# A transformer block with top-1 experts: token rows stored unsorted in f32 with their gate, and gathered by an inverse permutation made with one-hot matmuls

## What is computed

```python
mod = (_silu(L0_c) @ L0_wmod).reshape(L0_c.shape[0], 6, 1, -1)
sa, ca, ga, sb, cb, gb = (mod[:, 0], ...)          # ga, gb: size at least 0.25
h = _layernorm(x, axis=-1) * (1 + ca) + sa
x = x + ga * attention(h, Wqkv, bqkv, Wout, bout)
h = _layernorm(x, axis=-1) * (1 + cb) + sb
# feed-forward, on the 2048 rows of h:
logits = h @ router_w.T
scores = sigmoid(top-1 logit at its expert, -inf elsewhere)
xr = h[None, :, :] * scores.T[:, :, None]
gate, up = split(einsum('eth,ehf->etf', xr, gate_up_proj))
routed = einsum('etf,efh->eth', up * silu(gate), down_proj)
shared = silu(h @ shared_gate_w) * (h @ shared_up_w) @ shared_down_w
x = x + gb * (shared + routed.sum(axis=0))
```

## Time and profile before

| | us |
|---|---|
| median of 3 runs | 487.85 |
| profiled execution | 487.16 |
| its span, first to last instruction | 485.4 |
| TensorE busy | 401.1 (83%) |
| VectorE busy | 327.2 (67%) |
| GpSimd busy | 235.0 (48%) |
| ScalarE busy | 224.3 (46%) |

### The profile page before, as it was taken

One profiled execution on the slowest core, in us unless ns is written; L12 is line 12 of the kernel. 1 busy time (PEld: TensorE's weight loads), 2 busy tenths in 40 slices (PEclk: granted clock), 3 DMA queues, 4 the chain that ended last, 5 costly groups with the idle time before them and its releaser, 6 DMA issues.

```text
span 485.4 us, 8469 instructions
## 1 busy us (share of the span) xinstructions
PE 401.1 (83%) x2960; PEld 227.5 (47%) x2960; DVE 327.2 (67%) x619; ACT 224.3 (46%) x385; POOL 235.0 (48%) x267
## 2 busy tenths in 40 slices
PE   4738779899988999789986995777568999999991
PEld 4215335444654465444444452444345666666660
DVE  3779899557969879995678459959914444544431
ACT  2512325677566758466865661736601232222320
POOL 1482943653348713672247535428730555565542
PEclk9978999999999999999999999799969999999998
DMA  8563155736600663111222102518674343322320
GB/s 255 173 160 86 48 112 121 245 95 175 157 0 4 144 153 123 43 47 36 88 88 86 46 1 86 165 54 276 235 222 139 64 84 73 66 43 49 48 39 0
DMA packets 41319, 50.12 MB, mean 103 GB/s; under 512 B 5336, under 2 KB 36444, under 8 KB 41280
## 3 DMA queue, kind: packets, MB, share of 16 engines
q1 hardware_dynamic: 36096, 42.34, 30.5%
q0 software_dynamic: 5184, 7.25, 7.4%
HBM read 33.75 MB, written 16.75 MB: 104 GB/s over the span
## 4 chain that ended last, share of the span: by engine, by line
PE 55%; DVE 16%; POOL 8%; ACT 6%; DMA 6%; issue 6%; SPq 1%; DVEq 0%; POOLq 0%; ACTq 0%
PE bank L1341 33%; PE bank L1455 5%; PE bank L1439 5%; PE bank L1411 4%; DVE W L1115 3%; PE bank L1672 2%; DVE x_sb L1070 2%; DVE mx L1026 2%; POOL W L660 2%; ACT W L788 2%; PE bank L1413 2%; DMA boutb<-in_bout 1%; ACT W L813 1%; DMA qk_d<-W 1%; DVE W L1068 1%
## 5 line engine op out<-in xcount | busy, mean ns | idle before, releaser
L813 ACT ACTIVATE W<-bank 128x512 f32<-128x512 f32 (+1 forms) x176 | 95.0, 563 | 63.5 <-PE bank L1439 61.9
L1026 DVE TENSOR_REDUCE mx<-bank 128x1 f32<-128x384 f32 (+3 forms) x176 | 104.8, 631 | 22.8 <-PE bank L1413 22.2
L1341 PE MATMUL bank<-W 128*128 128x256 f16 (+2 forms) x756 | 108.0, 296 | 12.2 <-POOL W L654 3.4
L1341 PEld LDWEIGHTS bank<-W 128*128 128x128 f16 x756 | 74.2, 101 | 46.2 <-issue 12.4
L679 POOL TENSOR_SCALAR_AFFINE_SELECT W<-W 128x512 f32<-128x512 f32 x64 | 43.8, 687 | 83.0 <-ACT W L813 83.0
L1411 PE MATMUL bank<-W 126*128 126x128 f16 (+3 forms) x256 | 65.0, 309 | 14.0 <-DMA W<-qk_d 8.0
L1341 PE MATMUL bank<-W,h2T 128*128 x276 | 68.5, 385 | 1.3 <-issue 0.7
L1439 PE MATMUL bank<-W 128*128 128x512 f16 (+3 forms) x256 | 62.3, 304 | 2.5 <-ACT W L813 2.0
L756 POOL DMA_INDIRECT out<-h2T,row x23 | 36.4, 1582 | 56.8 <-DVE h2T L1310 56.5
L1455 PE MATMUL bank<-W 128*32 128x128 f32 (+3 forms) x512 | 47.5, 444 | 3.1 <-POOL W L679 3.1
L1341 PE MATMUL bank<-h2T,W 128*128 128x512 f16 x192 | 44.5, 384 | 5.2 <-DVE W L1130 5.2
(11 more groups left out here) (154 smaller groups left out, 560.6 us busy)
## 6 DMA issues: line engine op xcount, KB each, us to landing
stage<-in_gup SPq DMA_DIRECT2D x14, 512.0 KB
qk_d<-W SPq DMA_DIRECT2D x48, 128.0 KB
W<-qk_d SPq DMA_DIRECT2D x32, 192.0 KB, 4.2
stage<-in_down SPq DMA_DIRECT2D x7, 512.0 KB
row<-xs_d SPq DMA_DIRECT2D x23, 130.0 KB, 2.6
xs_d<-fillb SPq DMA_DIRECT2D x2, 1040.0 KB, 5.2
x_sb<-in_x SPq DMA_DIRECT2D x4, 512.0 KB, 9.0
out<-x_sb SPq DMA_DIRECT2D x4, 512.0 KB, 3.7
```

The lines of the kernel that those rows point to most:

```text
L813: a.activation(PT[j][:, i:i + m, :], t_bank(N)[:, 0:m * w].rearrange("p (i n) -> p i n", i=m), ACT.Exp).then_inc(s_exp, 1)
L1026: v.tensor_reduce(mx_v[:, b % 2, hp0 // 4, par, i:i + m, t], SB[N % 3][:, 0:m * w].rearrange("p (i n) -> p i n", i=m), AX.X, ALU.max).then ...
L1341: i = t_.matmul(outp, l, r, start=(n == 0), stop=(n == len(prods) - 1), **kw)
```

## The change

- Rows go to memory unsorted. A token's row in `h2_d` is 2 KB: 256 f32 values of h2 already multiplied by the sigmoid weight, and 256 f32 gate values gb. The gate halves of all rows are written once, in batch 0. The h2 halves are made by POOL (`rows`) in the attention loop, two batches behind, and by ACT for batch 3; SP stores them (`rows_out`).
- The weight of batches 0 to 2 is computed as 1 / (1 + exp(-top)) with ACT's exp and DVE (`expo`, `score`), that of batch 3 with the sigmoid as before.
- The high and low f16 parts of the rows, the zero fill, the 16 scatters, the loads of sorted tiles and the gathers of gates are gone. h2 is transposed in f32 (`h2_turn`), and its parts are made out of PSUM (`h2_high`, `h2_low`).
- `slots` makes, for every token, a one-hot of its tile (times its row number plus 1) and a one-hot of its row in the tile (`ohv`, `ohl`); 16 matmuls (`inverse`) turn them into the row number at every sorted place. `places` makes the gather and scatter indices. POOL then gathers the sorted tiles straight from `h2_d`, 8 buffers deep.
- In the routed stage two f32 transposes of a tile take the place of four f16 ones; ACT copies the high part (`rows_in_high`), DVE subtracts for the low one (`rows_in_low`).
- `POOL_UNITS` grows from 4 to 9 units, `ffn_splits` is another row of numbers, `hidden_low(n - 1)` stands right behind `hidden(n)`, and the jobs of batch 3 stand in another order.

```diff
-POOL_UNITS = (9, 11, 13, 15)
+POOL_UNITS = (9, 11, 13, 15, 17, 19, 21, 23, 25)
...
-        (27, "scale2", -1, 1), (28, "parts2", -1, 0), (29, "scale2", -1, 2), (29, "qk", 2, 2),
-        (30, "parts2", -1, 1), (31, "scale2", -1, 3), (31, "qk", 2, 3), (33, "parts2", -1, 2),
-        (35, "parts2", -1, 3), (20, "bias", 0, 0), (38, "h2", -1, 0), (40, "h2", -1, 1),
-        (42, "route", -1, 0)]
+        (27, "scale2", -1, 1), (29, "scale2", -1, 2), (29, "qk", 2, 2),
+        (31, "scale2", -1, 3), (31, "qk", 2, 3),
+        (20, "bias", 0, 0), (37, "h2", -1, 0), (39, "h2", -1, 1),
+        (42, "route", -1, 0), (2, "expo", -2, 0), (4, "score", -2, 0), (6, "rows", -2, 0), (8, "rows", -2, 1)]
...
-        row = sb("row", [P, NT, ROW], F16)
-        row32 = row[:, :, :].bitcast(F32)
+        rowg = sb("rowg", [P, RG, 2 * H])
+        o1 = rowg[:, 4:6, :].rearrange("p r (t n) -> p (r t) n", t=2)
+        h2f = o1
+        h2s = rowg[:, 6:8, :].rearrange("p r (t n) -> p (r t) n", t=2)
+        ohl = rowg[:, 0:2, :].rearrange("p r n -> p (r n)").bitcast(F16).rearrange("p (t n) -> p t n", t=NT)
...
-            return (2, 1, 1, 1, 1, 1, 2, 2, 2, 2, 2, 1)[n - FC * DEEP]
+            return (2, 2, 1, 2, 1, 1, 2, 2, 1, 2, 1, 1)[n - FC * DEEP]
...
+            def rows_out(b):
+                if b < B - 1:
+                    sp.wait_ge(s_rows, TT * (b + 1))
+                else:
+                    sp.wait_ge(s_rows3, TT)
+                sp.dma_start(h2_d[S * b:S * (b + 1), 0:H].rearrange("(t p) n -> p t n", p=P),
+                             h2s).then_inc(s_h2w, 16)
...
+                if b == 0:
+
+                    sp.wait_ge(s_gbb, 16)
+                    for c in range(B):
+                        sp.dma_start(h2_d[S * c:S * (c + 1), H:2 * H].rearrange("(t p) n -> p t n", p=P),
+                                     gbb[:, c].unsqueeze(1).to_broadcast([P, TT, H])).then_inc(s_gw, 16)
...
+                if b >= 2:
+                    rows_out(b - 2)
...
+                if n == 14:
+                    rows_out(B - 2)
+                if n == 23:
+                    rows_out(B - 1)
...
+            def rows(b, t):
+
+                n = TT * b + t
+                po.wait_ge(s_srow, b + 1)
+                if b and t == 0:
+                    po.wait_ge(s_h2w, 16 * b)
+                g.tensor_scalar(h2s[:, t], h2f[:, t], srow[:, n:n + 1], 0.0, ALU.mult, ALU.add).then_inc(s_rows, 1)
...
+            for t in range(TT):
+                rows(B - 2, t)
+            for n in (9, 11):
+                split_low(n)
             rstd(ve2, mv2, rs2, B - 1, s_mv2, s_rstd2)
             for t in (2, 3):
                 modulate2(B - 1, t)
-            for n in (11, 13, 15):
+            for n in (13, 15, 17, 19):
                 split_low(n)
...
-            po.wait_ge(s_pos, 1)
-            po.wait_ge(s_srow, 1)
-            po.wait_ge(s_fill, 16 * (B - 1))
-            for n in range(NT):
...
+            def gather(r):
+
+                if r >= RG:
+                    po.wait_ge(s_rye, r - RG + 1)
+                g.indirect_dma_start(rowg[:, r % RG, :], None, h2_d,
+                                     bass.IndirectOffsetOnAxis(ap=gidx[:, r:r + 1].bitcast(U32), axis=0)
+                                     ).then_inc(s_gr[r % RG], 16)
+
+            po.wait_ge(s_gi, 1)
+            po.wait_ge(s_gw, 16 * B)
+            po.wait_ge(s_h2w, 16 * B)
             for r in range(4):
-                gate_rows(r)
+                gather(r)
+            for n in (21, 23, 25):
+                split_low(n)
+            for r in range(4, RG):
+                gather(r)
+            po.wait_ge(s_si, 1)
             po.wait_ge(s_out, 16 * B)
             for r in range(RT):
 
                 po.wait_ge(s_rye, r + 1)
                 g.indirect_dma_start(out.rearrange("b s n -> (b s) n"),
-                                     bass.IndirectOffsetOnAxis(ap=row32[:, r % NT, 257:258].bitcast(U32), axis=0),
+                                     bass.IndirectOffsetOnAxis(ap=sidx[:, r:r + 1].bitcast(U32), axis=0),
                                      ry[r % YR], None, bounds_check=B * S - 1, oob_is_err=False,
                                      compute_op=ALU.add).then_inc(s_add[r % YR], 16)
-                if r + 4 < RT:
...
+                if r + RG < RT:
+                    gather(r + RG)
...
+            def h2_high(b, k):
+                ac.wait_ge(s_ht, 2 * b + k + 1)
+                a.activation(h2T[:, 0, k, S * b:S * (b + 1)], side_bank("h2", b, k)[:, :], ACT.Copy).then_inc(s_hta, 1)
+
+            def expo(b):
+                ac.wait_ge(s_top, b + 1)
+                a.activation(ex[:, TT * b:TT * (b + 1)], top[:, TT * b:TT * (b + 1)], ACT.Exp,
+                             scale=-1.0).then_inc(s_expo, 1)
+
+            def rows(b):
+                ac.wait_ge(s_h2w, 16 * b)
+                for t in range(TT):
+                    n = TT * b + t
+                    a.activation(h2s[:, t], h2f[:, t], ACT.Copy, scale=srow[:, n:n + 1]).then_inc(s_rows3, 1)
...
+                    ac.wait_ge(s_top, B)
+                    a.activation(srow[:, TT * (B - 1):NT], top[:, TT * (B - 1):NT], ACT.Sigmoid).then_inc(s_sg, 1)
+                    ac.wait_ge(s_sg, 1)
+                    rows(B - 1)
...
+                link(v.tensor_copy(pos_i[:, :], posr[:, :]))
+                link(v.tensor_scalar(pos_i[:, :], pos_i[:, :], ~(P - 1), None, ALU.bitwise_and))
+                link(v.tensor_copy(poshi[:, :], pos_i[:, :]))
+                link(v.tensor_tensor(poslo[:, :], posr[:, :], poshi[:, :], ALU.subtract))
+                link(v.tensor_tensor(ohh[:, :, :], itp[:, :].unsqueeze(1).to_broadcast([P, NT, RT]),
+                                     poshi[:, :].unsqueeze(2).to_broadcast([P, NT, RT]), ALU.is_equal))
+                v.tensor_tensor(ohv[:, :, :], ohh[:, :, :], idp[:, :].unsqueeze(2).to_broadcast([P, NT, RT]),
+                                ALU.mult).then_inc(s_pos, 1)
+                for c in range(0, NT, 4):
+                    v.tensor_tensor(ohl[:, c:c + 4], il[:, :].unsqueeze(1).to_broadcast([P, 4, P]),
+                                    poslo[:, c:c + 4].unsqueeze(2).to_broadcast([P, 4, P]),
+                                    ALU.is_equal).then_inc(s_ohl, 1)
...
+
+            def places():
+                ve.wait_ge(s_inv, 1)
+                inv = T1[:, H:H + RT]
+                v.tensor_scalar(gidx[:, :], inv, -1.0, 0.0, ALU.add, ALU.max).then_inc(s_gi, 1)
+                link(v.tensor_scalar(pad[:, :], inv, 0.5, float(OOB), ALU.is_lt, ALU.mult))
...
+                if n > FC * DEEP:
+                    hidden_low(n - 1)
...
-                if n == 9:
+                if n == 8:
+                    h2_low(B - 1, 0)
+                    h2_low(B - 1, 1)
+                    shared_out(1, 0)
                     logits(B - 1)
                     route()
-                    shared_out(1, 0)
+                    shared_out(1, 1)
+                if n == 9:
                     slots()
...
+                if n == 11:
+                    places()
+                    experts()
...
-                if n > FC * DEEP:
-                    hidden_low(n - 1)
...
+            def rows_in_low(r):
+                ve.wait_ge(s_rxh, r + 1)
+                v.tensor_tensor(xT[r % 2][:, H:2 * H], T0[:, 0:H], xT[r % 2][:, 0:H], ALU.subtract).then_inc(s_rxe, 1)
...
+                    pe.wait_ge(s_ye, TT * (b - 1) + 2 * (half + 1))
                 for t in (2 * half, 2 * half + 1):
-                    if b < DEEP:
-                        y = M1[:, H * (t % 2):H * (t % 2 + 1)]
...
             for n in range(FC * DEEP, NT):
+                if n == NT - 1:
+                    rows_turn(0)
                 shared_up(n)
...
                 if n == 8:
-                    pe.wait_ge(s_x2, TT * B)
+                    shared_down(1, 0)
                     h2_turn(B - 1, 0)
                     h2_turn(B - 1, 1)
+                    shared_down(1, 1)
+                    router(B - 1)
                 if n == 9:
-                    router(B - 1)
-                    shared_down(1, 0)
                     ranks()
-                if n == 10:
-                    shared_down(1, 1)
-                if n == 13:
+                if n == 11:
+                    inverse()
+                if n == 12:
                     shared_down(2, 0)
                     shared_down(2, 1)
```

282 lines of the change are left out of this document (122 added, 160 removed).

## The result

| | before | after |
|---|---|---|
| median of the runs, us | 488.01 (486.44 to 488.78) | 500.36 (499.79 to 501.44) |
| ratio, 95% interval | | 1.026 (1.023 to 1.029) |
| profiled run and its span, us | 487.16, 485.4 | 499.79, 498.0 |
| mean granted clock | 0.960 | 0.942 |

What follows compares the result with a forecast made beforehand. It took TensorE to bound the routed stage, while in the shared stage TensorE waits for VectorE and sorted rows. Terms -9.2 + 6.7 + 6 + 1.2 - 1.0 = +3.7 on 487.16 led to a forecast of 491.5 us, range 482.5 to 497.

Steps and rivals of the forecast that it cites:

- Tail gap: Last up block to end of down 3: the wait for scattered and reloaded rows goes, 19.2 to 9.95 us, -9.2 us.
- the count: VectorE requests that fall inside GpSimd operations, up to the one-hots, each waiting for its end: 10.5 us in all.
- the walk: Operations followed with profiled durations from up 5 to the end of down 3, first without collisions on VectorE.
- Collisions: Shared stage: VectorE operations reading two SBUF operands wait for GpSimd's splits, between 0 and 10.5 us, taken as +6 us.
- The shared stage grows: Up to the last up block: VectorE's new order and work delay TensorE, 353.4 against 346.7, +6.7 us without collisions.
- full collisions: Rival: every counted meeting of VectorE with GpSimd waits, all 10.5 us, +8.2 in sum, 496 us; chance 0.14.
- Routed stage: Two f32 transposes replace four f16 ones, +0.055 us in each of 22 tiles, +1.2 us; the new copy and subtract hide.
- Attention: Row copies and subtracts leave ScalarE and VectorE, GpSimd gets four products a batch: -1.0 us, bounds -4 and +1.
- the first sign: Sign of a right forecast: TensorE's 9.24 us wait, after the last up block, for the first sorted row tile is gone.
- late tile: Rival: the gathered tile is not there at up 15, costing 0 to 4 us on top; chance 0.06.
- routed chain: Rival: routed stage's copy and subtract chain doesn't fit, 0.2 us over per tile, +4.4 us, 496; chance 0.05.
- case without collisions: Rival: phases fall well or GpSimd yields, so VectorE loses nothing to speak of, -2.3 us, 485.5; chance 0.30.

Runs made afterwards that it cites:

- e2: The changed kernel with GpSimd filling the low halves of its nine units with zeros instead of computing them, so it reads nothing there: 480.7 us.
- e4: The changed kernel with VectorE's shared-out 2 moved from ahead of the last two splits and hidden-lows to behind the first row tile's subtract: 496.9 us.
- e6: The kernel before, with GpSimd filling the low halves of its four units with zeros instead of computing them: 480.6 us.
- e5: The changed kernel with no unit on GpSimd, VectorE making all eighteen late low halves: 492.8 us.
- e9: The kernel before, with no unit on GpSimd, VectorE making all eighteen late low halves: 479.8 us.
- e1: The changed kernel with only four units (9, 11, 13, 15) on GpSimd, the other five back on VectorE: 499.0 us.
- e3: The changed kernel with h2 transposes and router ahead of down 1 on TensorE, and logits and route ahead of shared-out 1 on VectorE: 499.2 us.

## Why the prediction was off

The profiled execution grew by 12.6 us, the forecast's sum was +3.7. Term by term:

- **Tail gap** (forecast -9.2, measured -1.5; error 7.7). This step failed. I named GpSimd's last split as what is late next, 2.5 us behind the last up block. It ended at 362.96 + 2.16 = 365.1, 2.8 us behind 362.35, but it was the wrong engine. VectorE's queue ended at 371.28, and the first gate half started 9.20 us behind the last up block. I never walked that queue behind hidden-low 11: split 22, hidden 13, then shared-out 2, splits 24 and 26, hidden 14 and 15, four hidden-lows (12 to 15) and the first row's subtract. e2 shows 4.71 us of the pause as that queue, e4 that taking shared-out 2 out of it moves the stage. The other 4.5 us are collisions at shared-out 2, which the count left out because it stopped at the one-hots. Against the 2.5 us that I had given it, the pause is 6.7 too long. The other 1.1 or so is the slow restart, for which I took 0.85 us: gate half and down took 2.74 and 6.01, together 8.5 us instead of 6.6, about what the earlier trace rows had shown (2.74 and 6.21). Even the place of GpSimd's last split came out right in part by luck. The durations that the prediction lists for it add up to 6.6 us from the start of up 14, about 1.1 us behind the end of up 15 and not 2.5; most of the rest is a wait that the walk did not have, ScalarE's for the load of unit 25:

```profile
360.69 1.06 ACT L885 ACTIVATE W<-stage 128x1024 f16<-128x1024 f32 x1 [0.98 <-DMA stage<-in_gup]
```

- **Collisions** (forecast +6, of a count of 10.5). The count was right: the extra time up to the one-hots is 3.2 + 2.1 + 5.0 = 10.3 us, at the three places that it named (3.4, 2.7 and 4.4 there). What failed was the choice of "a little over half". All the meetings of the earlier trace rows had waited in full, and I discounted the count because single phases were uncertain; they moved the three sums by 0.2 to 0.6 us, and the meetings were still paid in full. That is the rule of the Trainium skill (SBUF — State Buffer, section "Who interferes with whom"), that whichever is first holds the port for its whole length; the trace agrees with it here (331.79 against 331.77). The rival "full collisions", 496, was the nearest one.
- **The shared stage grows** (forecast +6.7). Together with the collisions the stage grew by 82.2 - 65.3 = 16.9, and 6.7 + 10.3 = 17.0. The walk of the order held within 1 us: the one-hots should have ended at 330.8, plus 10.3 for the waits, less 1.3 because up 4 starts that much sooner, which is 339.8, and they ended at 339.7. On the way two errors of 1 us cancelled. Down 1 started at 312.6 where the same working gives 309.6 + 5.3 - 1.3 = 313.6; the walk starts from before's times, which hold one of the waits already (0.9 us at 289.85), and the count has it again. The first half of down 1 then took 5.05 us and not 4.1.
- **Routed stage** (forecast +1.2, measured -1.6). The period is 4.62 us at first (388.12 to 392.74) against 4.68, 103.4 us from the first to the last hidden-turn against 103.8. I had added the difference of the transposes, though the f32 pair takes 0.38, the four 0.39; the product with a constant scale takes 0.68 instead of 0.75 us. From the last hidden-turn to the end it is 12.0 against 13.4 us. These 1.4 us lie behind the issue of the last scatter (5.6 against 6.9 us), and I can't explain them.

```profile
388.12 0.60 PE L1721 MATMUL bank<-ident,W 128*128 128x128 f32 x4
...
389.92 0.38 PE L1679 MATMUL bank<-ident,rowg 128*128 128x128 f32 x2
...
392.74 0.60 PE L1721 MATMUL bank<-ident,W 128*128 128x128 f32 x4
```

- **Attention** (forecast -1.0, measured -1.3 in this profile, about -1.0 as a mean of the table's first column). Right, within its scatter.

The errors, 7.7 + 4.3 - 0.1 - 2.8 - 0.3, are 8.8 of 8.9 us. Of the signs that the prediction named, most came: GpSimd's last split 2.8 us behind up 15, 7.53 us ahead of the inverse, an add of 1.90 us beside split 11. The pause ahead of down 1 was 8.71 us and not over 9, the period 4.62 and not 4.73. And the first sign, the 9.24 us gone, came true and said nothing, since another wait had its place. Two rivals are out: the first row transposes ran at 359.38 without a pause (late tile), and the routed period did not grow (routed chain). One share was also low: of the spread from 487.5 to 494.5 the part up to 490.3, within 0.5% of before, is 2.8 of 7 us and not a quarter; no term hangs on it.

One more thing was wrong, and didn't show in the sum. The forecast gave a case without collisions 485.5, a gain of 2.3 us. It set the changed kernel without collisions against before with its 4.4 us of them and its late scatters. With both rid of the splits' collisions, e2 against e6, there is no gain, though e2 is spared five splits more; with all splits made by VectorE, e5 against e9, the change loses 11 to 13 us in the order that it came in.

## What to carry to other kernels

When a change hands work from VectorE to GpSimd, charge VectorE for it: here nine splits of 1.14 us saved it 10.3 us and cost it 17.3 in waits (2.6 of them stood in before as well), and both kernels are faster with no unit on GpSimd (before by 7.4, after by 7.6 us). Before forecasting that a wait goes, walk the queue of every engine that the waiting instruction depends on down to that point, not only the queue that was changed. And try the cheap repair of the old kernel first: without units on GpSimd its wait for sorted rows, which the change was to remove, was 4.68 us instead of 9.24.

## What the runs showed of the hardware

- What a collision cost was set by what was left of GpSimd's operation, and not by the length of VectorE's. Operations on 8 and 16 columns, 0.17 us alone, took 1.98 us each behind GpSimd's 2.13 us. A chain of small dependent operations can meet GpSimd again at every link: in slots it did so four times, for 5.0 us.
- VectorE's operations with one operand in PSUM were not delayed: the residual's product (L1103) at 291.22 took 0.41 us inside GpSimd's operation from 291.11 to 293.28, which held up the add behind it (1.90 us at 291.67).
- The operation on 8 columns at 329.81 reads one SBUF operand (a tensor-scalar), which my count of operations with two had no reason to include. The Trainium skill (SBUF — State Buffer, section "Who interferes with whom") lists tensor-scalar among those that can take the shared port; the row agrees.
- A GpSimd fill, which only writes, delayed nothing: adds of two SBUF operands took 0.41 and 0.42 us beside fills from 299.01 to 299.99. The same section says that GpSimd's reads are what a second SBUF input contends with; the run agrees.
- GpSimd pays too: its second split operation took up to 2.98 us beside VectorE's work, 2.13 alone.
- A pause can cost twice. After 8.71 us half a down took 5.05 instead of 2.78, after 4.18 (in e1) a whole one 8.15, where before's took 5.41. Not every pause did: after 2.09 us down 2 took 7.08 in after, and after 1.74 us 5.42 in e3. In after the granted clock was 0.50 from 312 to 314 and from 372 to 374, the lower of the two levels (windows of after: length, busy us and instructions of PE, PEld, DVE, ACT and POOL, granted clock, DMA share, GB/s):

```profile
312.00:314.00 2.00, 1.37 (x7) 0.98 (x8) 0.57 (x1) 0.00 (x0) 0.00 (x0) 0.50 0.58 184
...
372.00:374.00 2.00, 2.00 (x6) 0.70 (x5) 0.00 (x0) 0.00 (x0) 0.00 (x0) 0.50 0.06 23
```
